# The score products of an attention head stacked in 96 contraction rows by DMA

## What is computed

```python
# layer A
nx = _ln(x, ln1_g, ln1_b)
q, k, v = nx @ wq + bq, nx @ wk + bk, nx @ wv + bv          # (b, h, s, 32)
scores = einsum('bhqd,bhkd->bhqk', q, k) / sqrt(HD) + bias  # bias: -inf where adj is 0
x1 = x + softmax(scores) @ v @ wo + bo
x = x1 + gelu(_ln(x1, ln2_g, ln2_b) @ w1 + b1) @ w2 + b2
# layer C
q, k, v = x @ Wq + bq, x @ Wk + bk, x @ Wv + bv
scores = where(adj == 0, -inf, einsum('bnhd,bmhd->bhnm', q, k) * scale)
y = x + softmax(scores) @ v @ Wo + bo
out = (y - mean(y)) * rsqrt(var(y) + EPS) * gamma + beta
```

## Time and profile before

| | |
|---|---|
| median of 3 runs | 2523.58 us (2523.16 to 2523.75) |
| profiled execution, span from first to last instruction | 2520.9 us |
| PE busy | 2363.7 us, 94% |
| VectorE busy | 2036.3 us, 81% |
| ScalarE busy | 1625.7 us, 64% |
| POOL busy | 1124.6 us, 45% |
| mean granted TensorE clock | 0.988 of full speed |
| DMA moved | 157.51 MB, 22.9% of 16 engines' time on SP's queue |

### The profile page before, as it was taken

One profiled execution on the slowest core, in us unless ns is written; L12 is line 12 of the kernel. 1 busy time (PEld: TensorE's weight loads), 2 busy tenths in 40 slices (PEclk: granted clock), 3 DMA queues, 4 the chain that ended last, 5 costly groups with the idle time before them and its releaser, 6 DMA issues.

```text
span 2520.9 us, 61217 instructions
## 1 busy us (share of the span) xinstructions
PE 2363.7 (94%) x17728; PEld 2006.7 (80%) x17728; DVE 2036.3 (81%) x8620; ACT 1625.7 (64%) x5518; POOL 1124.6 (45%) x1160
## 2 busy tenths in 40 slices
PE   5799999999999999999999999999999999999996
PEld 4688888888888888888888888788888788888875
DVE  4688888888888888888888888888888888888884
ACT  2467666667666667666667666667666667666764
POOL 1244454444454444454444454454453444443444
PEclk8899999999999999999999999999999999999998
DMA  4122221222221222212222212222212222212211
GB/s 123 34 70 62 67 55 54 65 75 61 67 53 56 65 75 61 67 50 59 65 75 61 67 49 60 65 75 61 67 47 62 65 75 61 67 46 63 58 47 40
DMA packets 172529, 157.51 MB, mean 62 GB/s; under 512 B 16832, under 2 KB 168000, under 8 KB 172352
## 3 DMA queue, kind: packets, MB, share of 16 engines
q1 hardware_dynamic: 172352, 155.91, 22.9%
HBM read 55.20 MB, written 16.78 MB: 29 GB/s over the span
## 4 chain that ended last, share of the span: by engine, by line
PE 47%; DVE 20%; issue 19%; ACT 13%; DVEq 1%; POOL 0%; ACTq 0%; POOLq 0%
PE p_bank L1025 26%; ACT scores L592 10%; PE p_scores L1025 9%; DVE hidden L836 6%; PE p_probs L1113 5%; PE p_bank L1127 4%; DVE hidden L838 3%; DVE x_two L704 3%; PE p_bank L1043 3%; DVE scores L789 2%; DVE res_a L870 1%; ACT hidden_raw L617 1%; DVE negmax L789 1%; DVE queries_a L813 1%; ACT hidden L609 1%
## 5 line engine op out<-in xcount | busy, mean ns | idle before, releaser
L542 POOL TENSOR_TENSOR scores<-scores,inverse 128x512 f32<-128x512 f32 x512 | 543.0, 1063 | 787.2 <-DVE inverse L799 787.0
L592 ACT ACTIVATE scores<-scores,negmax 128x128 f32<-128x128 f32 x2048 | 793.4, 391 | 103.8 <-DVE negmax L789 102.9
L1025 PE MATMUL p_bank<-w_down,hidden 128*128 128x256 f32 x3072 | 399.9, 286 | 26.7 <-DVE hidden L838 26.6
L1025 PEld LDWEIGHTS p_bank<-w_down,hidden 128*128 128x128 f32 x3072 | 379.5, 191 | 49.0 <-DVE hidden L838 39.4
L592 ACT ACTIVATION_READ_ACCUMULATOR scores<-scores,negmax 128x1 f32 x2048 | 387.4, 189 | 0.0
L1025 PE MATMUL p_bank<-normed,w_up 128*128 128x512 f32 x1536 | 366.7, 395 | 1.9 <-DVE normed L809 1.9
L1025 PEld LDWEIGHTS p_bank<-normed,w_up 128*128 128x128 f32 x1536 | 285.2, 189 | 61.1 <-issue 2.1
L629 ACT ACTIVATE heads_t<-p_bank 128x256 fp32r<-128x256 f32 x256 | 98.6, 385 | 308.2 <-PE p_bank L1127 308.1
L617 ACT ACTIVATE hidden_raw<-p_bank,ready_cols 128x512 f32<-128x512 f32 x256 | 173.4, 689 | 189.8 <-DVE hidden L838 128.4
L1113 PE MATMUL p_probs<-ident,scores 128*128 128x128 f32 x2048 | 273.2, 276 | 2.4 <-POOL scores L542 2.4
L1113 PEld LDWEIGHTS p_probs<-ident,scores 128*128 128x128 f32 x2048 | 228.6, 141 | 32.4 <-issue 19.8
(11 more groups left out here) (111 smaller groups left out, 4059.3 us busy)
## 6 DMA issues: line engine op xcount, KB each, us to landing
key_blocks<-hidden SPq DMA_DIRECT2D x512, 128.0 KB, 2.4
x_in<-in_x SPq DMA_DIRECT2D x32, 512.0 KB, 3.4
res_a<-in_x SPq DMA_DIRECT2D x32, 512.0 KB, 3.6
res_c<-x_two SPq DMA_DIRECT2D x32, 512.0 KB, 3.9
out<-res_c SPq DMA_DIRECT2D x128, 128.0 KB, 1.7
adj_a<-in_adj SPq DMA_DIRECT2D x32, 256.0 KB, 4.2
adj_c<-in_adj SPq DMA_DIRECT2D x32, 256.0 KB, 2.9
res_c<-in_L_gnn_w SPq DMA_DIRECT2D x1, 512.0 KB, 5.8
```

The lines of the kernel that those rows point to most:

```text
L542: nc.gpsimd.tensor_tensor(rows_c, rows_c, inverse[:, k % 2, heads].unsqueeze(2).broadcast_to([P, HC, P]), ALU.mult).then_inc(probs_made, 1)
L592: last = nc.scalar.activation(scores[:, k % 2, h], scores[:, k % 2, h], ACT.Exp, scale=-1.0, bias=negmax[:, k % 2, h:h + 1], accum_out=tot ...
L1025: last = nc.tensor.matmul(dst, stationary(i), moving(j), start=(n == 0), stop=(n == total_n - 1))
```

## The change

The two parts of keys and queries are now written to one buffer each, `flat_parts["K"]` and `flat_parts["Q"]`, shared by the two layers, and no longer inside `hidden`. SP copies both into stacks: for a head, the rows 0 to 31 of `query_stack` hold the high part, 32 to 63 the high part again and 64 to 95 the low part; `key_stack` holds high, low, high. One matmul over these 96 rows and 128 columns gives the three products of one head at once, so a unit has eight matmuls. A half of a group takes 3 x 4 copies for each of the two kinds, 24 of 32 rows x 2 x 256 values (64 KB). `copied` now stands before the writes of keys and of queries and no longer before those of `hidden`. The zero fill goes. The turns are all written out, each with fixed semaphore values.

```diff
+ROWS = {"Q": (HI, HI, LO), "K": (HI, LO, HI)}
+STACKED = len(ROWS["Q"]) * HD
+STACK_DMAS = len(ROWS["Q"]) * HC
...
-    for it, stages, following in [(0, "A", True), (1, "AM", True), ("loop", "AMC", True),
-                                  (NG - 1, "AMC", False), (NG, "MC", False), (NG + 1, "C", False)]:
-        before = Shape(it, stages, following, before, it in (0, NG, NG + 1))
+    for it in range(NG + 2):
+        stages = ("A" if it < NG else "") + ("M" if 1 <= it <= NG else "") + ("C" if it >= 2 else "")
+        before = Shape(it, stages, it < NG - 1, before, it in (0, NG, NG + 1))
...
-        queries = {"A": sb("queries_a", [P, 2, KC, TOK], F32R), "C": sb("queries_c", [P, 2, KC, TOK], F32R)}
-        key_blocks = sb("key_blocks", [P, KC, 2, HC, TOK], F32R)
+        flat_parts = {"Q": sb("queries", [P, 2, KC, TOK], F32R), "K": sb("keys", [P, 2, KC, TOK], F32R)}
+        stacks = {"Q": sb("query_stack", [P, KC, HC, TOK], F32R), "K": sb("key_stack", [P, KC, HC, TOK], F32R)}
...
-        keys = hidden[:, FC - KC:FC, :, :]
...
-        def copied(eng, t, before):
-
-
-            stage = {"A": "C" if t.s.c else "A", "C": "A" if t.s.a else "C", "M": "A" if t.s.a else "C"}[before]
+        def copied(eng, t, kind, before):
+
+            stage = {"A": "C" if t.s.c else "A", "C": "A" if t.s.a else "C"}[before]
             group = t.group_c + 1 if stage == "C" else t.group_a if before == "A" else t.group_a + 1
-            for blocks in blocks_loaded[stage]:
-                wait(eng, blocks, group * HC * 16)
+            for half_loaded in stacked[stage][kind]:
+                wait(eng, half_loaded, group * STACK_DMAS * 16)
...
-            def load_blocks(stage, half, condition):
-
-                sp.wait_ge(*condition)
+            def stack(t, stage, half, free=None):
+
                 two = slice(half * TOK // 2, (half + 1) * TOK // 2)
-                for j in range(HC):
-                    rows_j = slice(HD * j, HD * (j + 1))
-                    sp.dma_start(key_blocks[rows_j, :, :, j, two].bitcast(F32), keys[rows_j, :, :, two].bitcast(F32)
-                                 ).then_inc(blocks_loaded[stage][half], 16)
+                if free is not None:
+                    sp.wait_ge(scores_made, free * KC)
+                for kind in "KQ":
+                    for c in range(KC):
+                        sp.wait_ge(*drained_use(t, (kind, stage, c)))
+                    for r, part in enumerate(ROWS[kind]):
+                        for j in range(HC):
+                            sp.dma_start(stacks[kind][HD * r:HD * (r + 1), :, j, two].bitcast(F32),
+                                         flat_parts[kind][HD * j:HD * (j + 1), part, :, two].bitcast(F32)
+                                         ).then_inc(stacked[stage][kind][half], 16)
...
-                if s.a and s.before is not None:
-
-                    last_use = (masked_made, (unit0 + 2) * H) if s.c else drained_use(t, ("K", "A", 1))
-                    load_blocks("A", 0, last_use)
-                    load_blocks("A", 1, (masked_made, (unit0 + GB) * H) if s.c else last_use)
+                if s.a:
+
+                    stack(t, "A", 0, unit0 + 2 if s.c else None)
+                    stack(t, "A", 1, unit0 + GB if s.c else None)
...
-                    load_blocks("C", 0, drained_use(t, ("K", "C", 1)))
+                    stack(t, "C", 0, unit0 + len(s.order) - 2 if s.a else None)
...
-                    load_blocks("C", 1, (masked_made, (unit0 + len(s.order)) * H) if s.a
-                                else drained_use(t, ("K", "C", 1)))
+                    stack(t, "C", 1, unit0 + len(s.order) if s.a else None)
...
-            nc.gpsimd.memset(key_blocks[:, :, :, :, :].bitcast(F32), 0.0).then_inc(zeroed, 1)
...
-                        if kind == "K":
-
-                            copied(act, t, what)
+                        copied(act, t, kind, what)
...
-                        if j == FC - KC:
-                            copied(dve, t, "M")
...
                 for c in range(KC):
                     wait(pe, masked_made, u * H - H + HC * (c + 1))
-                    moving = lambda j: key_blocks[:, c, j, :, b * P:(b + 1) * P]
-                    stationary = lambda i: queries[stage][:, i, c, b * P:(b + 1) * P]
-                    three_passes(p_scores[:, c, :].rearrange("p (h n) -> p h n", h=HC), [(stationary, moving)]
-                                 ).then_inc(scores_made, 1)
+                    for j in range(HC):
+                        last = nc.tensor.matmul(p_scores[:, c, j * P:(j + 1) * P],
+                                                stacks["Q"][0:STACKED, c, j, b * P:(b + 1) * P],
+                                                stacks["K"][0:STACKED, c, j, b * P:(b + 1) * P], start=True, stop=True)
+                    last.then_inc(scores_made, 1)
```

More of the change, by code:

```diff
@@ L266, in build @@
         adj_loaded = {"A": sem("adj_a_loaded"), "C": sem("adj_c_loaded")}
-        blocks_loaded = {n: [sem(f"blocks_{n.lower()}_loaded{i}") for i in range(2)] for n in "AC"}
+        stacked = {n: {kind: [sem(f"stacked_{n.lower()}_{kind.lower()}{i}") for i in range(2)] for kind in "QK"}
+                   for n in "AC"}
         stored = sem("stored")
@@ L333, in build @@
         assert len(pieces) == len(staged) == len(piece_loaded)
-        ZEROED = 4
+        ZEROED = 3
         EARLY_VECTOR = 7
@@ L357, in setup_over @@
                     eng.wait_ge(drained[bank], number)
-        def copied(eng, t, before):
-            stage = {"A": "C" if t.s.c else "A", "C": "A" if t.s.a else "C", "M": "A" if t.s.a else "C"}[before]
+        def copied(eng, t, kind, before):
+            stage = {"A": "C" if t.s.c else "A", "C": "A" if t.s.a else "C"}[before]
             group = t.group_c + 1 if stage == "C" else t.group_a if before == "A" else t.group_a + 1
-            for blocks in blocks_loaded[stage]:
-                wait(eng, blocks, group * HC * 16)
+            for half_loaded in stacked[stage][kind]:
+                wait(eng, half_loaded, group * STACK_DMAS * 16)
         def split_part(kind, stage, part, c):
-            return queries[stage][:, part, c, :] if kind == "Q" else keys[:, c, part, :]
+            return flat_parts[kind][:, part, c, :]
         shapes = make_shapes()
@@ L433, in body @@
                 unit0 = t.grown(s.unit0, len(s.order))
-                if s.before is None:
-                    load_blocks("A", 0, drained_use(t, ("K", "A", 1)))
-                    load_blocks("A", 1, drained_use(t, ("K", "A", 1)))
                 if s.a and s.following:
@@ L491, in _ @@
             nc.gpsimd.memset(half[:, :], -0.5).then_inc(zeroed, 1)
-            nc.gpsimd.memset(key_blocks[:, :, :, :, :].bitcast(F32), 0.0).then_inc(zeroed, 1)
-            pool.wait_ge(zeroed, 3)
+            pool.wait_ge(zeroed, 2)
             nc.gpsimd.affine_select(out=ident[:, :], in_=ident[:, :], compare_op=ALU.not_equal, fill=1.0,
@@ L1091, in make_scores @@
                 u, stage, b = t.unit(s.steps.index(k))
-                if b == 0:
-                    for i in range(KC):
-                        bank, number = t.bank(("Q", stage, i), earlier=(stage == "C"))
-                        pe.wait_ge(drained[bank], number)
                 if b % 2 == 0:
-                    pe.wait_ge(blocks_loaded[stage][b // 2], (t.group(s.steps.index(k)) + 1) * HC * 16)
+                    for kind in "KQ":
+                        pe.wait_ge(stacked[stage][kind][b // 2], (t.group(s.steps.index(k)) + 1) * STACK_DMAS * 16)
                 for c in range(KC):
                     wait(pe, masked_made, u * H - H + HC * (c + 1))
-                    moving = lambda j: key_blocks[:, c, j, :, b * P:(b + 1) * P]
-                    stationary = lambda i: queries[stage][:, i, c, b * P:(b + 1) * P]
-                    three_passes(p_scores[:, c, :].rearrange("p (h n) -> p h n", h=HC), [(stationary, moving)]
-                                 ).then_inc(scores_made, 1)
+                    for j in range(HC):
[3 more added lines that the diff above has]
+                    last.then_inc(scores_made, 1)
             def lagging(t, op, r):
```

## The result

The changed kernel takes 2896.01 us (median of four runs, 2895.24 to 2904.49), the kernel before 2523.37 on the same chip: a ratio of 1.149, 95% interval 1.147 to 1.150. The forecast was 2834 us with a range of 2725 to 2945. Side, range and the main of the mechanism held; 62 us were missing.

What follows compares the result with a forecast made beforehand. TensorE was busy 2363.7 of 2520.9 us; SP's serial copy issue would then set the turn. 30 turns x 8.5 = +255, with +18.6, +15.5 and +22 about +310: 2834 us, range 2725 to 2945.

Steps and rivals of the forecast that it cites:

- the ring: ScalarE writes layer A's next first queries only after layer C's 48 copies leave the shared buffer; turn 84.2 us, +8.5.
- Copies of 0.646 us: SP's queue: 0.646 us from issue to issue whatever the copy's size; bounds 0.585 and 0.43.
- The stretch K C 1 to Q A 0: From layer C's last key drain to layer A's first query write: 48 copies, store and landing, 33.2 us against 22.4.
- PE's wait for C half 0: Scores of step 0 wait for the first 24 copies, 17.3 us after the key drain, inside the 33.2.
- From Q A 0 on: Rest of the turn, from layer A's first query write to layer C's last key drain: 53.3 us shrinks to 51.0.
- 2.3 us a turn back for the scores: Eight 128-column score matmuls replace six of 512 columns: 0.7 us saved per unit, 2.3 a turn on the chain.
- rival 1: The 128-column score matmul is slow, up to 0.258 us each: +108 us, 2942 us; chance 0.25.
- The written-out loop: PE's 1.34 us wait after a jump lies inside the copies' stretch: counted 0, worth up to 39 us if uncovered.
- A stacks hidden: Layer A's 48 copies end some 66 us after the key drain, covered by the long feed-forward step: 0.
- Rival 2: TensorE's clock falls after waiting for copies: 2.2 us a turn if all on the path, +66, near 2900; chance 0.10.
- Rival 3: SP issues copies fast enough, below 0.443 us each: 2504 us at 0.43, near 2455 with issue hidden; chance 0.07.
- The ends: Outside the 30 turn boundaries: start +18.6 us, turn 31 to 32 +15.5, last turn +22.

Runs made afterwards that it cites:

- own_queries_b: Changed kernel with a query buffer per layer and its own key buffer; w_down's low part overwrites its high part (values wrong): 2831.2 us, ratio 1.123.
- two_queues: Changed kernel with the 12 query copies of layer C's half 0 issued by ScalarE instead of SP, all computed: 2758.7 us, ratio 1.094.
- loop_only: Kernel before with only the loop written out: 2440.9 us, ratio 0.967.
- a_one_block: Changed kernel with one row block for layer A and three for layer C, 64 copies a turn instead of 96: 2879.2 us, ratio 1.141.
- warm_pe: Changed kernel with 40 and 8 extra matmuls filling PE's waits in steps 0 and 2, result unchanged: 2897.5 us, ratio 1.148.
- one_block: Changed kernel with one row block instead of three, 8 copies a half instead of 24, low-part products left out: 2401.5 us, ratio 0.952.

## Why the prediction was right, and where it was off

- **What closes the ring: half of it.** The prediction hangs the stretch on Q A 0 and the shared query buffer alone. C 2's scores wait for the same last copy (1492.05 and 1492.06), and with the buffer no longer shared own_queries_b keeps 308 of the 373 us. By either consumer the length is nearly the same (the turn is 84.0 there, 86.3 with both), so this did not show in the number.
- **Copies of 0.646 us, whatever their size: right.** In a run they start 0.64 apart, and 32 to 128 KB make no difference that matters.
- **The stretch K C 1 to Q A 0, 33.2 us: measured 34.4.** Four terms moved. Landing is 2.0 us, not 2.4 (-0.4). The store cost 1.0 instead of 0.39 (1473.50 to 1474.50, +0.6). And some issues take up to 2.0 us: 122 of 3072 are over 0.7, 91 us above the usual in all, 1.4 per 48 copies (+1.4). With the spacing of 0.64 (-0.3) this makes 34.5: errors of both signs, of which some cancel. Such issues were in the view of the kernel before (a maximum of 2115 ns) and were left out of the mean.
- **PE's wait for C half 0, 17.3: measured 18.2, inside the stretch: right.** (18.2 on this turn, 17.7 on the mean.) PE's own wait there is 9.14 us where 7 to 8 were forecast. two_queues shows how near it lay to being the bound.
- **From Q A 0 on, 51.0 us: measured 51.8.** This is the larger miss in kind. The sum gave 2.3 us a turn back for the scores; the rest shrank by 1.5, and loop_only has 0.7 of that without any new matmul. The group of scores was mis-sized: from its first matmul to the next instruction it takes 1.02 us (1446.21 to 1447.23, below), not the transposes' 0.79. The saving is 0.5 a unit, not 0.7. Single matmuls do start as the transposes do, in the trace every 0.112 us and every 0.109; what the group has more is 0.14 behind its first and 0.21 between its last and the value products. So rival 1, slow single matmuls of up to 0.258, did not happen. Its sum also left out the unit of step 2, which the forecast counts: at its bound it would be near 2978, not 2942.

PE of the changed kernel, step 5, beside the earlier trace rows:

```profile
1446.21 1.09 PE L1095 MATMUL p_scores<-key_stack,query_stack 96*128 96x128 f32 x8
1447.23 0.65 PE L1122 MATMUL p_bank<-probs_t,values_c 128*32 128x128 f32 x16
```

- **The written-out loop counted at nothing: right in place, low in price.** Inside the copies' stretch it saved nothing that could be seen, since that stretch has the copies' length. The price if uncovered was put at up to 39 us (1.3 x 29; the turns 2 to 30 have 28 jumps between them); alone it is 82.5. So against its true competitor, the kernel before with a written-out loop, the stacks cost 455 us and not 373.
- **A stacks hidden: right** (a_one_block). **Rival 2: what speaks for it is seen, and it costs at most 0.3 us a turn here** (warm_pe); in two_queues it seems to cost more. **Rival 3 did not happen**; but its condition could be met from the other side: one_block (32 rows) gives 2401.5, which is how fast the scheme is once issue is hidden, beside the forecast of about 2455; 82 of those 122 us are the loop's.
- **The ends.** Start +19.5 against +18.6. From the last full turn to the end +30.9 against 15.5 + 22; where those 6.6 us went was not taken apart.
- **The sum.** 19.5 + 30 x 10.7 + 30.9 = 371, against 310 forecast. A turn grew by 10.7 instead of 8.5: 1.2 in the copies part, 0.8 in the rest, and 0.2 because the mean turn before is 75.56 and not the looped turn's 75.7. In 30 turns that is 66 us, of which the ends give some 6 back.

What stays open: why the written-out loop also gains 0.7 us a turn far from the jump, what the low clock costs once the copies' wait is shorter, and how the scheme would do with SP's issues spread over two queues from the first copy on, which was not tried. The block scheme of before with the written-out loop (loop_only, 2440.9 us) is the fastest kernel here that computes all.

## What to carry to other kernels

Count DMAs by the time that their queue needs to issue them, before counting bytes: here a queue gives one such SBUF copy in 0.64 us, be it of 32 or 128 KB, and 48 in a row are 31 us that no matmul saving of half a microsecond a unit pays back. Ask of each run of copies which buffer or product waits for its last one, and of each edit that comes with another what it does alone: the loop was worth 82 us and was invisible in the sum. When a wait is relieved, look for the next one behind it before counting the gain, as two_queues did not gain its 12 x 0.64 = 7.7 us a turn but 4.3.

## What the runs showed of the hardware

**Long DMA issues beside instruction fetches.** In the changed kernel's chain one issue of a run takes 1.89 us instead of 0.60:

```profile
1460.02 0.60 SPq L429
1460.66 1.89 SPq L429
```

In that microsecond the instruction queue moves 16 KB (DMA queues between 1459 and 1462 us: packets, MB, share):

```profile
q8 instruction: 1, 0.02, 3.3%
```

The same coincidence stands at 1392.87, 1427.39 and 1483.29 us. Over the whole trace 109 of the 3072 copies have an issue of over 0.9 us, and 108 of these have a packet of that queue between 1 us before their start and 0.5 us after their end; of the 2950 of at most 0.7 us, 163 have one. The kernel before, with its loop, has 4 issues of over 0.7 us in 512 copies, loop_only 21 in 512. So the written-out kernel has more of the long issues; that the fetch is their cause was not tested by itself.

**The 128-column matmul of the rounded type** over 96 rows, with a fresh stationary side, starts every 0.112 us inside a group of eight, where the 128-column transposes start every 0.109; a group takes 1.02 us against 0.79 until the next instruction starts. The 81 ns of the Trainium skill ("TensorE: Matmul & The Clock Gate", Back-to-back issue gap) is not reached by either.

**The jump of a hardware loop** with this many engines in step costs 2.8 us a turn here (75.75 against 72.93). 1.6 of them lie where VectorE begins the next turn late: C 0's scores and the first key product are 4.58 us apart, 2.99 with the loop written out.
